# A gated state-space block in which the log part of softplus gets a second buffer

## The reference, cut to what matters

```python
xn = _ln(xh, norm_w, norm_b)
p = xn @ w_in.T
x1, x2 = (p[..., :C], p[..., C:])
u = x1 @ ssm_in_w.T
xss, z = silu(u[..., :C]), silu(u[..., C:])
xd = einsum('bhwd,kcd->bhwkc', xss, x_proj_w)
dtr, Bv, Cv = ranks, B and C of xd
dt = softplus(einsum('bhwkr,kdr->bhwkd', dtr, dt_w) + dt_b)
bc = sum(Bv * Cv, axis=-1)
gain = sum(bc[..., None] * dt + Ds, axis=-2)
y = _ln(xss * gain, out_norm_w, out_norm_b) * z
x = x + (y @ ssm_out_w.T * silu(x2) @ w_out.T)
```

## Time and profile before

| what | value |
|---|---|
| median of 3 runs | 5588.4 us (5583.93 to 5594.35) |
| the profiled execution | 5583.01 us, span 5581.2 us |
| busy share of the span: PE, DVE, POOL, ACT | 86%, 80%, 72%, 51% |
| first block, by the step loop | about 62 to 555 us of the span |
| busy in 115.4 to 465.2 us (349.8 us): PE, ACT, DVE, POOL | 318.3, 264.0, 232.6, 157.0 us |

### The profile page before, as it was taken

How to read it: one execution, slowest core, us unless ns; L and a number is a source line. 1 busy time by engine, 2 the same in 40 slices (tenths; PEclk the granted TensorE clock), 3 DMA queues, 4 the chain that set the end, 5 groups by cost and what they waited for, 6 DMA issues and landing times. The chain is left out here.

```text
span 5581.2 us, 73628 instructions
## 1 busy us (share of the span) xinstructions
PE 4818.2 (86%) x15882; PEld 2217.7 (40%) x15882; DVE 4480.0 (80%) x4834; ACT 2849.1 (51%) x4454; POOL 4043.3 (72%) x2760
## 2 busy tenths in 40 slices
PE   7998898995799999993788888888888888888887
PEld 2333464661366666662442222222222222232222
DVE  3666434335179999899769999999999999999996
ACT  5775444342111111110237777777777777777776
POOL 2444423233169898989669999999999999999993
PEclk9998999997899999996889999999999999999998
DMA  2000000007768787772417777676777777767773
GB/s 51 1 0 6 2 1 0 1 0 232 188 123 153 137 150 137 146 145 37 97 34 187 186 187 187 186 187 187 187 187 183 187 187 186 188 186 188 188 187 96
DMA packets 373865, 711.78 MB, mean 128 GB/s; under 512 B 76669, under 2 KB 111657, under 8 KB 359369
## 3 DMA queue, kind: packets, MB, share of 16 engines
q1 hardware_dynamic: 373576, 708.57, 52.5%
HBM read 575.73 MB, written 82.32 MB: 118 GB/s over the span
## 5 line engine op out<-in xcount | busy, mean ns | idle before, releaser
L2098 POOL TENSOR_TENSOR l_hc<-l_h,l_c_rep 128x512 f32<-128x512 f32 x1536 | 1929.6, 1275 | 201.3 <-DVE l_h L2152 173.3
L2152 DVE TENSOR_TENSOR_SCAN l_h<-l_p_da,l_h,l_bu 128x512 f32<-128x512 f32 x1120 | 1406.0, 1272 | 1.2 <-ACT l_p_da L2003 0.4
L2003 ACT ACTIVATE l_p_da<-l_p_da,l_a_neg 128x512 f32<-128x512 f32 x1536 | 1008.6, 658 | 719.5 <-PE l_p_da L1858 704.5
L1304 POOL TENSOR_TENSOR l2b_prod<-l2b_v,l2b_attn 128x1568 f32<-128x1568 f32 x276 | 937.9, 3451 | 240.7 <-DVE l2b_osum L1352 123.4
L1858 PE MATMUL l_p_da<-l_stacked,l_pick 96*128 96x512 f32 x1536 | 909.6, 594 | 182.6 <-DVE l_h L2152 176.8
L2137 DVE TENSOR_TENSOR l_bu<-l_du_rep,l_p_b 128x512 f32<-128x512 f32 x1280 | 845.2, 660 | 28.0 <-DMA l_du_rep<-du_scratch 22.9
L1858 PEld LDWEIGHTS l_p_da<-l_stacked,l_pick 96*128 96x128 f32 x1536 | 293.7, 192 | 1152.6 <-DVE l_h L2152 886.4
L1352 DVE TENSOR_REDUCE l2b_osum<-l2b_prod 128x32 f32<-128x1568 f32 x384 | 665.7, 1780 | 63.2 <-POOL l2b_prod L1304 59.5
L1866 PE MATMUL l_p_y<-l_hc,l_y_pick 128*32 128x512 f32 x3072 | 565.4, 628 | 73.6 <-POOL l_hc L2098 73.6
L1257 ACT ACTIVATE l2b_logits<-l2b_conv,l2b_this_b 98x512 f32<-98x512 f32 x96 | 66.2, 689 | 869.3 <-PE l2b_conv L1222 869.3
L1222 PE MATMUL l2b_conv<-l2b_img_high,l2b_w_conv_high 128*98 128x512 f32 x1344 | 357.8, 420 | 38.5 <-DMA l2b_img_low<-qkv_scratch 38.5
(11 more groups left out here) (265 smaller groups left out, 8688.6 us busy)
## 6 DMA issues: line engine op xcount, KB each, us to landing
l_du_rep<-du_scratch SPq DMA_DIRECT2D x1536, 256.0 KB, 3.9
l2b_img_high<-qkv_scratch SPq DMA_DIRECT2D x192, 306.2 KB, 5.6
l2b_img_low<-qkv_scratch SPq DMA_DIRECT2D x192, 306.2 KB, 9.4
l_stacked<-l_parts SPq DMA_DIRECT2D x512, 96.0 KB, 2.7
l2b_v<-v_scratch SPq DMA_DIRECT2D x192, 152.0 KB, 6.6
qkv_scratch<-l2a_strip SPq DMA_DIRECT2D x32, 840.0 KB, 5.1
du_scratch<-l_du SPq DMA_DIRECT2D x128, 192.0 KB, 2.2
v_scratch<-l2a_v_strip SPq DMA_DIRECT2D x32, 228.0 KB, 4.1
```

The costliest lines, as they stand in the source:

```text
L1304: return eng.tensor_tensor(dst.rearrange("q x (dy dx) -> q x dy dx", dx=WIN), window, attn_half[:, :, unit % 2].rearrange("q x (dy dx) -> ...
L2003: act.activation(p_da[i % DAS][:], p_da[i % DAS][:], ACT.Exp, scale=a_neg[:, k * G + GRP[i]:k * G + GRP[i] + 1]).then_inc(s_da, 1)
L2098: pool.tensor_tensor(hc[:, (G * par + i) % HCS, :], h[:, i, :], c_rep[:, par, :], ALU.mult).then_inc(s_hc, 1)
L2152: dve.tensor_tensor_scan(h[:, i, way], p_da[i % DAS][:, way], of, state, ALU.mult, ALU.add).then_inc(s_h, 1)
```

## The change

`log_part` gets a second buffer, chosen by the parity of the tile, as `dt` has it. `dt_abs(m, k)` now waits for `add_log(m-2, k)`. `dt_exp`, `dt_log` and `add_log` index the buffer of their tile. No instruction is added, removed or moved on any engine; the buffer takes 3 x 512 x 4 = 6144 bytes more of each partition while the block runs.

```diff
-        log_part = sb("l0_log_part", [128, CHUNKS, N])
+        log_part = sb("l0_log_part", [128, 2, CHUNKS, N])
...
             def dt_abs(m, k):
                 act.wait_ge(s_relu, CHUNKS * m + k + 1)
-                if m:
-                    act.wait_ge(s_dt, CHUNKS * (m - 1) + k + 1)
-                act.activation(log_part[:, k, :], p_chunk[k], ACT.Abs, bias=dt_bias[:, k:k + 1]).then_inc(s_abs, 1)
+                if m >= 2:
+                    act.wait_ge(s_dt, CHUNKS * (m - 2) + k + 1)
+                act.activation(log_part[:, m % 2, k, :], p_chunk[k], ACT.Abs, bias=dt_bias[:, k:k + 1]).then_inc(s_abs, 1)
...
-                act.activation(log_part[:], log_part[:], ACT.Exp, scale=-1.0).then_inc(s_exp, 1)
+                act.activation(log_part[:, m % 2], log_part[:, m % 2], ACT.Exp, scale=-1.0).then_inc(s_exp, 1)
...
-                act.activation(log_part[:], log_part[:], ACT.Ln, bias=1.0).then_inc(s_log, 1)
+                act.activation(log_part[:, m % 2], log_part[:, m % 2], ACT.Ln, bias=1.0).then_inc(s_log, 1)
...
-                pool.tensor_tensor(of, of, log_part[:, k, :], ALU.add).then_inc(s_dt, 1)
+                pool.tensor_tensor(of, of, log_part[:, m % 2, k, :], ALU.add).then_inc(s_dt, 1)
```

## The result

| | kernel before | changed kernel |
|---|---|---|
| median | 5589.1 us (5583.9 to 5594.4, 4 runs) | 5547.0 us (5542.5 to 5547.6, 4 runs) |
| ratio, 95% interval | | 0.9923 (0.9906 to 0.994) |
| profiled execution, its span | 5583.0 us, 5581.2 us | 5546.6 us, 5544.8 us |
| 23 regular steps and 6 groups of projections | 349.8 us | 310.2 us |
| first block, first L391 to last L360 | 483.1 us | 433.0 us |

A forecast was written before the change was run, and what follows sets the result against it. PE was taken to be near its limit in the first block, losing time to waits in a POOL-ACT-PE chain and the slower clock behind them. 38.7 + 7.9 + 1.6 = 48.2 us off 5588.4 gave 5540 us, range 5529 to 5560.

The forecast's parts named there:

- The double price of a wait: First block's steps: PE's wait costs idle time (1.38 us) and a slower clock behind it; a slow step takes 4.65 us more.
- What is late next: DVE's `gains` reading the tile POOL adds to: POOL finishes 0.55 us ahead, so slow steps should become full-speed steps.
- The rule on shared ports: DVE's L381 while POOL works: counted at 0.78 us instead of 0.40; the rule could hold it for a whole addition.
- DVE as the new bound: Rival, chance 0.12: L381 held up for a whole addition, 0.67 us a step, 15 us given back, 5555 us.
- The clock rival: Rival, chance 0.10: the clock keeps falling in the steps, only the 23.5 us of waits are saved, 5565 us.
- The regular steps, 38.7 us: 23 steps and 6 groups of projections, 349.82 us: all become full-speed at 10.84 us a step, 311.1 us, saving 38.7.
- The last steps, 7.9 us: Five last steps with norms, 55.37 us: each takes 9.49 us, 47.5 in all, saving 7.9 us.
- The early steps, 1.6 us: Early steps: PE's waits of 0.61 and 0.95 us in one step go, clock left as it is, saving 1.6 us.
- The sum, 48.2 us: First block: 38.7 + 7.9 + 1.6 = 48.2 us saved, later blocks unchanged; forecast 5540 us, chance 0.71.

The follow-up runs named there:

- the reordered POOL program: Kernel before with one buffer, POOL's third addition moved ahead of its product with z: 5546.4 us, ratio 0.9921 to the kernel before.
- the first pair: The first profile of each kernel, before and changed: profiled executions of 5583.0 and 5546.6 us, first blocks of 483.1 and 433.0 us.
- second and third profile of the kernel before: The kernel before, unchanged, profiled twice more: first block 475.2 and 480.4 us, regular steps 346.8 and 346.9 us.
- the first timing: The changed kernel first timed against the kernel before: 5547.0 against 5589.1 us, ratio 0.9923.

## Why the prediction was right

- *The double price of a wait.* Shown. The forecast took PE's idle time and the clock behind it as one thing; the work put into the wait removed the falls in the regular steps, while ACT's wait stayed.
- *What is late next.* Right: `gains` never waits for `add_log`, whose third instruction ends at 278.44 us, when DVE is in its second chunk. The 0.55 us of room were enough, and POOL does not slip further in the steps that follow each other.
- *The rule on shared ports.* L381 takes 0.77 us in such steps, as the 0.78 that was counted, and DVE still has 0.41 us idle behind it. SBUF — State Buffer, "Who interferes with whom", in the Trainium skill allowed it to be held for a whole addition; the trace agrees with the rule in kind, since both take longer where they meet (L381 0.77 us against 0.40, the third L453 1.46 us against 1.25 for each of the first two), but a hold-up of a whole instruction shows nowhere in these steps. DVE as the new bound did not happen.
- *The clock rival.* Wrong for the regular steps: with the 0.6 us wait left in each of the 23, the clock is 1.00 in three profiles of three. TensorE: Matmul & The Clock Gate, "A second HAM failure mode: psum-queue depth-cycling", in the Trainium skill states that short, frequent idle pieces of PE can make the clock swing; these traces agree for pieces of 1.4 us and 0.6 together, and in the regular steps not for 0.6 alone, nor for the 0.43 us by which ACT was late in the reordered POOL program. The forecast left one thing out: among the last steps pieces of 0.15 to 0.35 us were followed by a fall in one profile of three, at a price of 1.4 us.
- *The regular steps, 38.7 us.* Measured 39.6 in the first pair; 36.6 and 36.7 with the second and third profile of the kernel before.
- *The last steps, 7.9 us.* 55.37 us before; 421.94 to 469.78 us, so 47.84, after: 7.5 in the first pair. The mean of three profiles each is 55.0 and 48.3: 6.7.
- *The early steps, 1.6 us.* From the first L391 to the first L142 are 39.2 us before and 35.3 after in the first pair, so 3.9: the forecast left the clock there as it was, but a fall behind those two waits went as well. In the mean of three profiles each it is 2.6 (38.3 and 35.7); in one of the three of the kernel before that fall did not come.
- *The sum, 48.2 us.* 50.1 us in the first block of the first pair, 46.1 in the mean of three profiles each, 42.0, 50.6 and 44.6 in the timings. That the first pair comes so near to 48.2 is in part luck: the sum was sized on an execution with more falls of the clock than the two others; this, and later blocks that vary by 10 us of themselves, is the distance from the first timing. The mechanism stands.

## What to carry to other kernels

Price a wait of the matmul engine by the length of its steps and not by the idle time alone: here 23.5 us of waits cost about 46, because the clock fell behind about half of them. Before a buffer is doubled, see which piece of it is waited for, and behind what it stands on its engine: one chunk of three, or another order on POOL, gave nearly the same. When steps of equal work come in two lengths, the count of the short ones gives the gain quite well, but take more than one profile, as the number of long ones may vary.

## What the runs showed of the hardware that was not expected

- Work of no use can be free: 112 matmul passes, 48 us, put where PE waited left the time at 0.9997 (0.9988 to 1.0006), for they fill its waits and the clock then stays at 2.4 GHz in the regular steps.
- Equal waits, of 1.36 and 1.37 us in steps of the same shape, are followed by a fall of the clock in one case and by none in the other, and the number of falls in unchanged code went from 10 to 12 between executions. With them the first block moves by up to 8 us.
- The selective scan, untouched, takes 2567 to 2578 us from one execution to the next, with no difference between the kernels.
